# Two fused attention layers on one core: value copies, low-part splits and one MLP product moved at the seams

## The reference

```python
# layer 0: latents = x, h = [context, x]; 16 heads of 32
q = latents @ q_w + q_b
k, v = split(h @ kv_w + kv_b)
attn = softmax(where(mask, q . k / 32, -inf))
o = (attn @ v) @ out_w + out_b + latents
o = o * rsqrt(mean(o * o) + 1e-6) * postnorm_w
x1 = gelu(o @ mlp_w1 + mlp_b1) @ mlp_w2 + mlp_b2 + latents
# layer 1: hidden = x1, keys and values from layernorm(context)
Q, K, V = x1 @ Wq.T, ln(context) @ Wk.T, ln(context) @ Wv.T
out = x1 + tanh(gate) * (softmax(Q . K * 32 ** -0.5) @ V) @ Wo.T
```

## Time and profile before

| what | value |
|---|---|
| median of the runs | 2311.32 us |
| the profiled execution, its own time | 2312.23 us |
| its span, first to last instruction | 2310.4 us |
| PE busy in the span | 2278.0 us (99%) |
| ACT busy | 1432.6 us (62%) |
| DVE busy | 1063.7 us (46%) |
| POOL busy | 420.0 us (18%) |
| mean granted TensorE clock | 0.991 |

### The profile page before, as it was taken

One profiled execution on the slowest core, in us unless ns is written; L12 is line 12 of the kernel. 1 busy time (PEld: TensorE's weight loads), 2 busy tenths in 40 slices (PEclk: granted clock), 3 DMA queues, 4 the chain that ended last, 5 costly groups with the idle time before them and its releaser, 6 DMA issues.

```text
span 2310.4 us, 42833 instructions
## 1 busy us (share of the span) xinstructions
PE 2278.0 (99%) x14366; PEld 1873.6 (81%) x14366; DVE 1063.7 (46%) x1942; ACT 1432.6 (62%) x3378; POOL 420.0 (18%) x522
## 2 busy tenths in 40 slices
PE   9999999999999999899999999999999999999998
PEld 7777888888888887688888888888888888888886
DVE  7555555555555555532112112112165655656563
ACT  5777777777777777643222222222257878787786
POOL 4222222222222223300000000001022121211110
PEclk9999999999999999899999999999999999999998
DMA  7444444444444444341011011012055555655553
GB/s 216 112 120 119 118 112 112 117 119 119 119 119 119 119 118 99 101 146 55 1 54 54 0 54 54 0 54 91 1 166 135 149 140 140 148 136 152 130 130 89
DMA packets 141971, 239.12 MB, mean 103 GB/s; under 512 B 25393, under 2 KB 59601, under 8 KB 139873
## 3 DMA queue, kind: packets, MB, share of 16 engines
q1 hardware_dynamic: 140512, 238.05, 38.9%
q10 hardware_dynamic: 1408, 0.41, 0.1%
HBM read 86.28 MB, written 25.21 MB: 48 GB/s over the span
## 4 chain that ended last, share of the span: by engine, by line
PE 54%; ACT 1%; DVE 1%; DMA 1%; SPq 0%; issue 0%; DVEq 0%
PE item_ps L66 7%; PE item_ps L68 6%; PE item_ps L67 6%; PE score_ps L67 5%; PE score_ps L66 5%; PE score_ps L68 5%; PE o_ps L66 4%; PE o_ps L68 4%; PE o_ps L67 4%; PE score_ps L1435 3%; PE score_ps L1408 3%; PE o_ps L1451 2%; PE item_ps L1289 1%; ACT score_ps L850 1%; SPq L535 0%; DMA layer_result<-rows 0%
## 5 line engine op out<-in xcount | busy, mean ns | idle before, releaser
L850 ACT ACTIVATE score_ps<-score_ps,l_neg_max 128x512 f32<-128x512 f32 (+1 forms) x1024 | 566.3, 556 | 187.1 <-DVE l_neg_max L1094 183.1
L1094 DVE TENSOR_REDUCE l_neg_max<-score_ps 128x1 f32<-128x512 f32 (+1 forms) x768 | 496.9, 684 | 97.4 <-PE score_ps L1408 95.2
L1884 ACT ACTIVATE mlp_hidden<-score_ps,b_col 128x512 f32<-128x512 f32 x128 | 88.2, 689 | 498.7 <-PE score_ps L68 453.8
L1932 DVE TENSOR_TENSOR mlp_hidden_l<-mlp_hidden,mlp_hidden_h 128x512 fp32r<-128x512 f32 x128 | 92.9, 726 | 513.5 <-ACT mlp_hidden_h L1886 513.4
L66 PE MATMUL item_ps<-feats_h,weights_l 128*128 128x256 f32 (+1 forms) x1024 | 323.5, 316 | 2.7 <-POOL feats_l L705 1.1
L67 PE MATMUL item_ps<-feats_l,weights_h 128*128 128x256 f32 (+1 forms) x1024 | 317.2, 310 | 0.0
L68 PE MATMUL item_ps<-feats_h,weights_h 128*128 128x256 f32 (+1 forms) x1024 | 316.9, 309 | 0.0
L1408 PE MATMUL score_ps<-l_stack 97*128 97x512 f32 (+1 forms) x1024 | 295.0, 353 | 7.0 <-DMA l_stack<-l_qk 3.1
L870 ACT ACTIVATE l_probs<-score_ps 128x1024 f32<-128x1024 f32 x272 | 269.2, 1024 | 33.1 <-PE score_ps L1435 26.9
L1435 PE MATMUL score_ps<-l_stack 99*128 99x256 f32 x1536 | 249.1, 292 | 2.7 <-ACT score_ps L850 1.1
L1435 PEld LDWEIGHTS score_ps<-l_stack 99*128 99x128 f32 x1536 | 214.2, 192 | 46.1 <-issue 29.2
(11 more groups left out here) (165 smaller groups left out, 4032.1 us busy)
## 6 DMA issues: line engine op xcount, KB each, us to landing
l_stack<-room SPq DMA_DIRECT2D x254, 192.0 KB, 3.2
l_stack<-l_qk SPq DMA_DIRECT2D x254, 128.0 KB, 2.4
l_stack<-room SPq DMA_DIRECT2D x130, 128.0 KB, 2.9
l_tokens<-in_features SPq DMA_DIRECT2D x16, 1024.0 KB, 4.8
l_stack<-l_qk SPq DMA_DIRECT2D x254, 64.0 KB, 2.1
l_stack<-room SPq DMA_DIRECT2D x130, 64.0 KB, 3.0
l_rows<-in_x SPq DMA_DIRECT2D x16, 512.0 KB, 3.3
norm_transposed<-norm_room SPq DMA_DIRECT2D x16, 512.0 KB, 2.7
```

The costliest lines, as they stand in the source:

```text
L850: m = act.activation(e, e, ACT.Exp, bias=neg_max[:, q, h:h + 1], accum_out=row_sum[:, q, h:h + 1])
L1094: dve.tensor_reduce(out, bank, AXIS_X, ALU.max, negate=True).then_inc(max_done, 1)
L1884: act.activation(hidden[:, m % HBUF, :], hidden_ps[:, m % 4, :], ACT.Gelu_apprx_tanh, bias=b1_col[:, m:m + 1])
L1932: dve.tensor_tensor(hidden_p[1][:, m % HBUF, :], hidden[:, m % HBUF, :], f32(hidden_p[0][:, m % HBUF, :]), ALU.subtract).then_inc(hidden_l ...
```

## The change

In layer 0's last batch VectorE's four value copies, which stood together after step 19, stand one by one after steps 9, 13, 16 and 20; the first shift is made after step 20 instead of 19, turned after 23 instead of 21 and copied after 22 instead of 20; `turn_norm` of the batch before stands after step 26 instead of 25. On VectorE `o_low(0)` and `o_low(1)` stand before `first_lows` and before the four `w1_low`. TensorE's first MLP product stands before the last projection instead of after it. In layer 1, in all 16 batches, the two value copies go from ScalarE (ahead of step 8's sum) to VectorE (behind step 8's maximum and ahead of `make_shift(a, 0)`).

```diff
-    V_COPIES_IN_SLOT = {2: (0,), 3: (1,), AFTER_T: (2, 3)} if first else {}
+    V_COPIES_IN_SLOT = {2: (0,), 3: (1,), AFTER_T: (2, 3)} if first else {AFTER_T: (0, 1)}
...
-        SHIFT_MADE_AT, SHIFT_TURNED_AT, SHIFT_COPIED_AT, NORM_TURNED_AT = 19, 21, 20, 25
-        V_OF_ACT = [] if first else list(range(KB))
+        SHIFT_MADE_AT, SHIFT_TURNED_AT, SHIFT_COPIED_AT, NORM_TURNED_AT = 20, 23, 22, 26
+        V_COPIED_AT = {9: 0, 13: 1, 16: 2, 20: 3}
+        V_OF_ACT = []
...
             def last_first_pass_of_four_keys(a):
                 for k in range(AHEAD, STEPS):
                     step_max(a, k)
+                    if k in V_COPIED_AT:
+                        copy_v(a, V_COPIED_AT[k])
                     if k == SHIFT_MADE_AT:
-                        for t in range(KB):
-                            copy_v(a, t)
                         make_shift(a, 0)
...
                     if p is not None:
                         low(p, MIXED)
-                    else:
+                    o_low(a, 0)
+                    if p is None:
                         ahead.first_lows(dve)
+                    o_low(a, 1)
+                    if p is None:
                         for part in range(FB):
                             ahead.parts.w1_low(dve, 1, part)
-                    o_low(a, 0)
-                    o_low(a, 1)
...
                 groups_of_four_keys(None, a, run, shifted)
+                ahead.parts.up(pe, 0, 0)
                 project(a, 3)
...
             if first:
-                ahead.parts.up(pe, 0, 0)
                 ahead.parts.up(pe, 0, 1)
                 turn_norm(B - 1, last=True)
```

## The result

| what | before | after |
|---|---|---|
| median of the runs, us | 2311.28 (7 runs) | 2319.22 (7 runs) |
| ratio, 95% interval | | 1.0037 [1.0027, 1.0047] |
| the profiled execution, us | 2312.23 | 2320.91 |
| its span, us | 2310.4 | 2319.1 |
| PE, DVE, ACT busy, us | 2278.0, 1063.7, 1432.6 | 2283.3, 1071.9, 1420.7 |

The changed kernel is slower by 0.37%, 8.6 us with an interval of 6.2 to 10.9 (the ratio times 2311). Forecast were 2317.4 us and slower with a chance of 0.60. The median lies 1.8 us above the forecast and inside the range of 2309.5 to 2320.5.

The account below looks back on a forecast made before the run. PE is busy 99% of the span, so only idle time and the lower clock can move. -2.3 - 4.4 + 1.5 + 1.6 + 9.7 = +6.1 us: 2318.3, or 2317.4 for the median; range 2309.5 to 2320.5.

Parts of the forecast that it names:

- Layer 1's loop, +9.7: Layer 1's loop: copies on DVE delay step 9's maximum and item 7 by 0.69 us in 14 batches, +9.7 us.
- hidden: Rival: layer 1 hides the copies as ACT has less work; the 9.7 is 0, total 2307.7 us, chance 0.14.
- half absorbed copies: Rival: PE comes later to item 7 for another reason; +4.9 instead of 9.7, total 2312.6 us, chance 0.10.
- The tail, +1.5: Layer 0's tail: the moved MLP product starts turn_norm 1.5 us later, with PE idle 2.6 us ahead of it.
- the clock behind it, +1.6: Layer 0's tail: behind the new 2.6 us gap PE runs 3.2 us at half clock, costing 1.6 us.
- The copies and the shift, -2.3: Layer 0's last batch: copies between steps let the last exponential and the first weigh come 2.3 us earlier.
- The low parts, -4.4: Layer 0's last batch: o_low(0) goes first; saves 2.5 us wait, 1.6 half clock behind it, 0.3 the rest.
- Layer 1's first batch, 0: Layer 1's first batch: fewer steps stand in that slot, so no cost; bounds -0.3 to +0.5 us.
- The last batch, 0: Layer 1's last batch: the shift is turned at 2281.24 again, so no cost; bounds -0.9 to +0.3 us.

Follow-up runs that it names:

- experiment 1: Only layer 1's value copies moved to DVE, layer 0 as in the kernel before: 2321.36 us beside 2313.48, ratio 1.0036.
- Experiment 7: Kernel before, but in layer 1 one value copy on DVE and the other on ACT: 2312.92 us, ratio 0.9999.
- Experiment 8: Changed kernel, but layer 1's two copies two DVE instructions earlier, ahead of item 3's low part: 2305.92 us beside 2311.23 for the kernel before, ratio 0.9975.
- experiment 2: All of layer 0's edits, layer 1 as in the kernel before: 2309.08 us, ratio 0.9985.
- experiment 4: Kernel before with only the first MLP product moved before the last projection: 2315.24 us beside 2311.23, one execution.
- experiment 6: Kernel before with only layer 0's copies step by step and the shift and turn_norm later: 2312.32 us beside 2311.23, one execution.
- experiment 3: Layer 0's edits without the moved MLP product, layer 1 as in the kernel before: 2308.40 us, ratio 0.9977.
- experiment 5: Kernel before with only o_low(0) and o_low(1) put ahead of the MLP's low parts: 2310.56 us beside 2311.23, one execution.
- experiment 9: Changed kernel, but MLP product left behind the projection and layer 1's copies ahead of item 3's low part: 2301.59 us beside 2312.82 for the kernel before, ratio 0.9955.

## Why the prediction came out as it did

**Layer 1's loop, +9.7: right, in mechanism and in size.** The traces have +9.7 between the marks and 0.65 to 0.70 us a batch (the change and experiment 1). From shift to shift, 13 distances are 0.70 us longer and the first and the last of the 15 by 0.33 and 0.35. One detail was off: the prediction put 0.15 us of a batch's delay at the turned shift and the rest ahead of item 7, as an idle gap of about 0.7. The stalls are 0.34 us at each of the two places (0.46 from start to start, less 0.12), and the view shows 0.18 of idle time for either. Experiment 7 shows that the delay counts from the point at which step 9's maximum comes behind ACT's own pace. Experiment 8 shows that ACT's load (418.71 us in the loop against 304.51 of DVE) decides nothing: the same move wins or loses by where it lands. The loss of 9.7 us in the loop, and the 8.3 us of experiment 1, rule out the rivals of hidden and of half absorbed copies.

**The tail, +1.5, and the clock behind it, +1.6: right.** In the two traces +1.53 (last `weigh` to `turn_norm`, 11.63 against 10.10) and +1.58 (`turn_norm` to the mark, 5.76 against 4.18). PE was granted 0.50 behind the gap of 2.66 us, as behind the 2.53 of before; after, that was from about 979.3 to 982.4, so it began 1 us behind the gap's end. By the Trainium skill, "TensorE: Matmul & The Clock Gate", section "Why this matters for your kernels", this gap is shorter than those it warns of; the trace and experiments 2 and 4 disagree, and the measurement decides.

**The copies and the shift, -2.3: right in size, with two things missed.** In the two traces the first `weigh` is 1.81 us earlier; the mean of the five traces without this edit is 950.48, that of the five with it and the low parts 948.10, so -2.4. But the shift was turned at 935.23 and not at 934.65, since the small instructions of `make_shift`, for which I took 0.17 us each, had become longer:

```profile
933.96 0.16 DVE L1102 TENSOR_TENSOR l_log_sum<-l_neg_max,l_log_sum 128x16 f32<-128x16 f32 x1
934.16 0.31 DVE L1104 CAST l_shift<-l_log_sum 128x16 fp32r<-128x16 f32 x1
934.50 0.63 DVE L1106 TENSOR_TENSOR l_shift<-l_log_sum,l_shift 128x16 fp32r<-128x16 f32 x1
```

And this gain is worth next to nothing by itself (experiment 6): the term stands only with the next one beside it.

**The low parts, -4.4: right in mechanism, up to 0.5 too much.** From the first to the last `weigh` are 22.61 us before and 18.73 after, -3.9. The wait and the half clock behind it are gone. The 0.3 that denser work was to get back isn't seen in this pair: the first `weigh` took 3.64 us as before. But this stretch differs from one execution to the next by more than that: 20.19 to 23.69 us in the five traces with the low parts as before (mean 22.5), 17.74 to 18.73 in the six with them moved (mean 18.4), and the first `weigh` took 2.72 to 3.64, by how far the half clock reached into it. A size to a tenth can't be had from one pair.

**Layer 1's first batch, 0: too low, by 0.2 to 1 us.** Experiments 1 and 2 differ here only in who copies, and run alike up to the copies (first scores to the DMA wait 9.80 and 9.75 us). With the copies on DVE:

```profile
1710.77 0.71 PE L1408 MATMUL score_ps<-l_stack 97*128 97x256 f32 x4 [1.23 <-DMA l_stack<-l_qk]
...
1725.36 0.28 PE L1420 MATMUL o_ps<-ident_r,l_shift 128*16 128x128 f32 x2 [0.72 <-DVE l_shift L1105]
```

With the copies on ACT:

```profile
1706.76 0.71 PE L1410 MATMUL score_ps<-l_stack 97*128 97x256 f32 x4 [1.24 <-DMA l_stack<-l_qk]
...
1720.40 0.28 PE L1422 MATMUL o_ps<-ident_r,l_shift 128*16 128x128 f32 x2
```

14.59 us to the turned shift against 13.64: the copies cost 0.95 us here, more than in a batch of the loop, and the prediction had bounded it by +0.5. In the three other traces in which the clock stayed at 1.00 here (experiments 3, 6 and 7, with at most one copy on DVE) it is 13.44 to 13.69.

In the changed kernel's own trace most of the first batch's +1.67 us is something else. There the clock is at 0.50 from 1710 to 1716, before only from 1712 to 1714, and PE has no wait for the shift. The same stretch took 15.53 us after, and 15.28, 15.28 and 15.36 in experiments 5, 8 and 9, which have about 6 us at 0.50 there, too, but not this place for the copies (experiment 5 has layer 1 as before). So where the clock falls the copies cost some 0.2 us, and about 1.4 of the 1.67 came with the clock and not with the edit. The wait for the first queries and keys ahead of this batch was 1.23 to 2.93 us in the eleven traces, with no relation to the edits. Behind waits of 1.23 to 1.25 us (experiments 1 to 3) the clock stayed at 1.00. Behind 2.27 and 2.29 it stayed there in experiments 6 and 7, and behind 2.27 it fell in 5 and 8; behind 2.70 and more it fell each time. Why a DMA lands late in some executions stays open.

**The last batch, 0: right.** PE waits 2.05 us for the shift and turns it at 2289.95, 8.71 later than before, which is what had come together by then.

The sum was +6.1 and the difference measured 8.6 [6.2, 10.9]. In the two traces the terms are -1.8, -3.9, +1.5, +1.6, +9.7, +1.7 for the first batch and -0.1 for the rest, +8.7. The median was forecast 1.8 us too low. In the traces the excess stands in the first batch (mostly its clock) and in the low parts and copies; but the medians of the kernel before lay between 2311.2 and 2313.5 us in the four sets of executions, so a difference of 1.8 can't be put down to a term.

## What to carry to other kernels

Before work goes from a fuller engine to an emptier one, look for the instruction behind it that the next engine waits for: by the traces the same two copies cost 9.7 us ahead of a maximum on the chain and gained some 4 us in the idle time two instructions earlier. To fill a hole of 1.1 us with 2.7 us of work that was the cover of a later wait moves the hole and makes it larger. A gain at one wait has to be followed to the next fixed one (here the low parts in front of `o_low(0)`), and edits that lie in a row on one chain are tried together as well as alone.

## What the runs showed of the hardware

**DVE's small instructions beside POOL.** POOL's instructions of 1.57 us (weights, TENSOR_SCALAR) follow each other every 1.54 us, so the third began at 934.41 in the after trace:

```profile
931.33 6.19 POOL L114 TENSOR_SCALAR weights_h<-room,norm_w 128x512 fp32r<-128x512 f32 x4 [6.98 <-DMA room<-in_L_xattn_mlp_w]
```

The last shift instruction ended at 935.13, 0.72 us behind that start. In the traces of experiments 1 to 6, 8 and 9 it ended 0.70 to 0.72 us behind such a start, with a length of 0.56 to 0.63 us. In six of these and after, the CAST ahead of it was longer as well (0.22 to 0.49 us instead of 0.17). Before and in experiment 7 the last shift instruction fell away from any start and took 0.17. By the Trainium skill, "SBUF — State Buffer", section "Who interferes with whom", a DVE instruction with two inputs in SBUF contends with a POOL instruction that reads SBUF; the traces fit that, and here it came free 0.7 us into POOL's 1.57. No kernel was run with POOL's work taken away, so the cause is read from the phases and not shown by an experiment.

**The clock behind short gaps.** Behind the gap of 2.66 us in the tail PE ran at 1.2 GHz for some 3 us in each of the four kernels with the moved product (5.5 to 5.8 us to the mark instead of 4.18). Where it began differed: after, `turn_norm` took 1.09 us as at full clock and the products behind it were slow, while in experiment 4 `turn_norm` itself took 1.97. Behind a gap of 1.1 us (the projection, in experiments 3 and 5) the clock did not fall. Behind gaps of 2.27 to 2.29 us at the start of layer 1 it fell in two traces and stayed at 1.00 in two others, so a gap's length alone doesn't decide it in these traces.
